# Down-projection by one level of Strassen's scheme, the feed-forward in two passes of 256 tokens, keys and values kept in DRAM

## The reference, cut to what matters

```python
q = layer_norm(query, ln1_g, ln1_b)
qh, kh, vh = split(q @ wq + bq), split(context @ wk + bk), split(context @ wv + bv)
scores = where(allowed, qh kh^T / sqrt(32), -inf)         # 64 context rows
o = softmax(scores) vh
x = query + o @ wo + bo
h = layer_norm(x, ln2_g, ln2_b)
out = x + gelu(h @ w1 + b1) @ w2 + b2                     # w1 512x2048, w2 2048x512
```

## Time and profile before

| | us |
|---|---|
| median of three runs | 1868.11 (1867.82 to 1868.26) |
| span of the profiled execution, the only time that the page gives of it | 1864.5 |
| PE busy in it | 1799.3 (97%) |
| DVE busy | 1247.9 (67%) |
| ACT busy | 640.5 (34%) |
| POOL busy | 443.8 (24%) |

### The profile page before, as it was taken

One profiled execution on the slowest core, in us unless ns is written; L12 is line 12 of the kernel. 1 busy time (PEld: TensorE's weight loads), 2 busy tenths in 40 slices (PEclk: granted clock), 3 DMA queues, 4 the chain that ended last, 5 costly groups with the idle time before them and its releaser, 6 DMA issues.

```text
span 1864.5 us, 26584 instructions
## 1 busy us (share of the span) xinstructions
PE 1799.3 (97%) x10213; PEld 819.6 (44%) x10213; DVE 1247.9 (67%) x1930; ACT 640.5 (34%) x799; POOL 443.8 (24%) x376
## 2 busy tenths in 40 slices
PE   6678899999999999999999999999999999999999
PEld 3233344444444444444444444444444444444444
DVE  6767757667675767757676676757677576866622
ACT  5654424242232424223242422324242232424211
POOL 2523114131320314122141313203141221413200
PEclk8878999999999999999999999999999999999999
DMA  8230232314123241412323131332413133231200
GB/s 288 54 105 12 46 91 46 91 23 79 35 60 77 46 91 23 78 36 57 80 46 91 19 81 38 57 80 46 91 21 77 40 57 79 46 91 19 50 23 23
DMA packets 287738, 116.27 MB, mean 62 GB/s; under 512 B 262616, under 2 KB 264192, under 8 KB 287616
## 3 DMA queue, kind: packets, MB, share of 16 engines
q1 hardware_dynamic: 287616, 114.61, 27.4%
HBM read 31.22 MB, written 16.78 MB: 26 GB/s over the span
## 4 chain that ended last, share of the span: by engine, by line
PE 90%; DVE 5%; POOL 1%; ACT 1%; DMA 1%; issue 1%; SPq 0%; DVEq 0%; ACTq 0%
PE ff_ps L1141 34%; PE ff_ps L1384 34%; PE at_ps L1141 18%; PE at_ps L1298 2%; PE at_ps L1318 1%; DVE w_all L829 1%; POOL arena L560 1%; DVE arena L829 0%; DVE xhat L818 0%; DMA arena<-in_L_xattn_wk 0%; PE ff_ps L1213 0%; DVE arena L1114 0%; DVE arena L1061 0%; PE at_ps L1213 0%; DVE smax L1059 0%
## 5 line engine op out<-in xcount | busy, mean ns | idle before, releaser
L1141 PE MATMUL ff_ps<-arena,w_all 128*128 128x512 f16 x3072 | 701.8, 381 | 2.3 <-DVE arena L829 2.3
L1384 PE MATMUL ff_ps<-w_all,arena 128*128 128x512 f16 x3072 | 698.0, 379 | 0.9 <-DVE arena L829 0.9
L1141 PEld LDWEIGHTS ff_ps<-arena,w_all 128*128 128x128 f16 x3072 | 300.4, 98 | 371.7 <-issue 15.6
L1384 PEld LDWEIGHTS ff_ps<-w_all,arena 128*128 128x128 f16 x3072 | 294.4, 98 | 358.6 <-issue 6.4
L753 ACT ACTIVATE arena<-ff_ps,b1p,scales 128x512 f32<-128x512 f32 x256 | 198.5, 775 | 634.6 <-PE ff_ps L1141 634.3
L1114 DVE TENSOR_SCALAR arena<-arena,scales 128x512 f16<-128x512 f32 x256 | 150.1, 586 | 215.6 <-ACT arena L753 215.5
L829 DVE SCALAR_TENSOR_TENSOR arena<-arena,scales 128x512 f16<-128x512 f32 x256 | 239.2, 934 | 9.1
L511 POOL TENSOR_TENSOR rstd<-ve,minus_half 128x1 f32<-128x1 f32 x128 | 85.6, 669 | 561.1 <-DVE ve L801 561.1
L555 POOL TENSOR_TENSOR x_sb<-x_sb,bo_row 128x512 f32<-128x512 f32 x64 | 92.6, 1477 | 359.8 <-PE at_ps L1298 350.5
L687 ACT ACTIVATE norm_hl<-xhat 128x512 f16<-128x512 f32 x120 | 73.9, 628 | 287.6 <-DVE xhat L818 287.6
L560 POOL TENSOR_TENSOR arena<-arena,rsum 128x1024 f32<-128x1024 f32 x64 | 124.8, 1971 | 176.1 <-DVE rsum L1087 176.1
(11 more groups left out here) (154 smaller groups left out, 1377.3 us busy)
## 6 DMA issues: line engine op xcount, KB each, us to landing
x_sb<-in_x SPq DMA_DIRECT2D x64, 256.0 KB, 2.8
out_x<-arena SPq DMA_DIRECT2D x64, 256.0 KB, 2.1
w_all<-in_L_xattn_w SPq DMA_DIRECT2D x6, 1024.0 KB, 11.6
arena<-in_L_xattn_w SPq DMA_DIRECT2D x2, 1024.0 KB, 15.8
v_sb<-v_sb SPq DMA_DIRECT2D x6, 192.0 KB, 3.0
arena<-in_ctx SPq DMA_DIRECT2D x1, 1024.0 KB, 5.2
arena<-in_L_xattn_wk SPq DMA_DIRECT2D x1, 1024.0 KB, 7.4
arena<-in_L_xattn_wq SPq DMA_DIRECT2D x1, 1024.0 KB, 7.4
```

The lines of the kernel that those rows point to most:

```text
L1141: last = nc.tensor.matmul(out_ap, s, m, start=(i == 0), stop=(i == n - 1))
L1384: last = nc.tensor.matmul(ff2_ps[:, t, :], pair[:, s, rows], m[:, j], start=(j == 0 and i == 0), stop=(j == NJ - 1 and i == 2))
```

## The change

A group of the feed-forward is now two feature tiles by 256 tokens instead of one tile by 512. FF1 of a group is 24 matmuls of 256 columns. Four blocks of 128 x 128 (two tiles, two halves of the 256 tokens) come out of the gelu, which is two ACT instructions of 256 columns into blocks 0, 2, 4, 6 of `comb`. DVE adds three pairs of blocks and subtracts two, so that seven blocks stand there (896 columns); ACT makes their high half by a Copy, DVE their low half. FF2 of a group is the seven products of Strassen's scheme, each of three matmuls with 256 columns: 21 matmuls in the place of 24 of that width. The seven sums gather in four banks, and DVE puts them into the residual by eight instructions for each 256 tokens (`update`), 16 for each slot. The first pass of a slot (groups 0 to 7) is for its first 256 tokens, the second for the others.

w2 is brought in eight pieces of two row blocks into a ring of two stages, POOL adds and subtracts its blocks, and ACT and DVE convert seven blocks of 128 x 256 for each piece, in slot 1, at the positions of `CONV_SECOND_AT`. Its maxima are taken earlier in slot 0. Keys and values go to DRAM in slot 0, and in each odd slot SP loads those of the next batch (six DMAs); the POOL steps that built `kblk` and copied the values are gone but for slot 0. The attention of slots 2 to 15 is planned four positions earlier, with the steps in the same order; slot 1 keeps the old plan.

```diff
 LAG = 3
-GROUPS = NJ + LAG
+NGROUP = NJ
+GROUPS = NGROUP + LAG
+SUBS = 2
+PAIRS = NJ // 2
+SUB = CHUNK // SUBS
+DH = D // 2
+NPROD = 7
+PRODUCTS = ((2, 6, 0, 0), (4, 0, 0, 1), (6, 5, 1, 0), (5, 4, 1, 1), (1, 2, 2, 0), (0, 1, 2, 1), (3, 3, 3, 0))
 PLAN = {
+    3: [("Q", 0), ("Q", 1), ("Q", 2), ("Q", 3)],
+    4: [("S", 0)], 6: [("S", 1)], 7: [("E", 0), ("E", 1)], 8: [("S", 2)],
+    9: [("U", 0), ("U", 1)], 10: [("S", 3)],
+    11: [("Z", 0), ("Z", 1), ("L", 0), ("L", 1), ("E", 2), ("E", 3)],
+    12: [("U", 2), ("U", 3)],
+    14: [("Z", 2)], 15: [("Z", 3), ("L", 2), ("L", 3)],
+    19: [("V", 0), ("V", 1)], 20: [("V", 2), ("V", 3)],
+    21: [("O", 0), ("O", 1)],
+    22: [("G", 0), ("O", 2), ("G", 1), ("D", 0), ("O", 3), ("G", 2), ("D", 1), ("G", 3), ("D", 2), ("D", 3)],
+    23: [("N", 0), ("N", 1), ("N", 2), ("N", 3)],
+    25: [("A", 0), ("A", 1), ("C", 0), ("A", 2)], 26: [("C", 1), ("A", 3), ("C", 2)], 27: [("C", 3)],
+}
+PLAN_LATE = {
...
-W2_SUMS_AT = (19, 20, 21, 22)
+W2_SUMS_AT = (11, 12, 17, 18)
+CONV_SECOND_AT = {1: (12, 13), 2: (14,), 3: (15, 16), 4: (17,), 6: (18, 19), 8: (20, 21), 9: (22, 23),
+                  10: (24, 25), 12: (26, 27), 14: (28, 29), 16: (30, 31), 18: (32, 33), 20: (34, 35)}
...
+            def load_values(batch):
+                for half in (slice(0, SC), slice(SC, P)):
+                    sp.dma_start(v_now[half], v_batches[batch].rearrange("k (a n) -> k a n", a=2)
+                                 ).then_inc(kv_loaded, 16)
+            def load_keys(batch):
+                for q in range(GH):
+                    rows = slice(q * HD, (q + 1) * HD)
+                    sp.dma_start(kblk[rows, :, :, q % 2, :].rearrange("p a g k -> p (a g) k"),
+                                 k_batches[batch, rows, :, :]).then_inc(kv_loaded, 16)
...
+                    if ff:
+                        store_out(c, par, 0)
+                    if par and loads:
+                        sp.wait_ge(v_ps, 4 * c + TT)
...
+                        load_keys(ahead)
+                        load_values(ahead)
...
+                def add_w2(j):
+                    w = stage[j % 2]
+                    pool.wait_ge(w2_staged[j % 2], 32 * (j // 2 + 1))
+                    nc.gpsimd.tensor_tensor(w[:, 1:6:2, :], w[:, 0:5:2, :], w[:, 2:7:2, :], ALU.add
+                                            ).then_inc(pool_adds, 1)
+                    pool.wait_ge(pool_adds, j + 1)
+                    nc.gpsimd.tensor_tensor(w[:, 0:7:6, :], w[:, 0:3:2, :], w[:, 4:7:2, :], ALU.subtract
+                                            ).then_inc(w2_added, 1)
...
# ACT, group g
-                        nc.scalar.activation(gelu_full[g % 2], ff1_ps[:, g % 2, :], ACT.Gelu,
-                                             bias=b1p[:, g:g + 1], scale=col(C1)).then_inc(g_full, 1)
+                        for y in range(2):
+                            ft = 2 * (g % PAIRS) + y
+                            last = nc.scalar.activation(
+                                comb[g % 2][:, 2 * y:2 * y + 5:4, :],
+                                ff1_ps[:, g % 2, y * SUB:(y + 1) * SUB].rearrange("p (m n) -> p m n", n=P), ACT.Gelu,
+                                bias=b1p[:, ft:ft + 1], scale=col(C1))
+                        last.then_inc(g_full, 1)
+                    if ff and 1 <= g <= NGROUP:
+                        act.wait_ge(g_comb, NGROUP * c + (g - NGROUP))
+                        nc.scalar.activation(g_pair[(g - 1) % NG][:, 0], comb[(g - 1) % 2], ACT.Copy, scale=col(SG)
+                                             ).then_inc(g_hi, 1)
...
# DVE, group g
-                        nc.vector.tensor_scalar(pair[:, 0, :], gelu_full[g % 2], col(SG), None, ALU.mult
-                                                ).then_inc(g_hi, 1)
-                        dve.wait_ge(g_hi, NJ * c + (g + 1 - NJ))
-                        low(pair[:, 1, :], gelu_full[g % 2], col(SG), pair[:, 0, :], g_lo)
+                        w = comb[g % 2]
+                        nc.vector.tensor_tensor(w[:, 1:6:2, :], w[:, 0:5:2, :], w[:, 2:7:2, :], ALU.add
+                                                ).then_inc(g_sums, 1)
+                        dve.wait_ge(g_sums, NGROUP * c + (g + 1 - NGROUP))
+                        nc.vector.tensor_tensor(w[:, 0:7:6, :], w[:, 0:3:2, :], w[:, 4:7:2, :], ALU.subtract
+                                                ).then_inc(g_comb, 1)
+                    if ff and 1 <= g <= NGROUP:
+                        dve.wait_ge(g_hi, NGROUP * c + (g - NGROUP))
+                        pair = g_pair[(g - 1) % NG]
+                        low(pair[:, 1], comb[(g - 1) % 2], col(SG), pair[:, 0], g_lo)
+                    if ff and g == PAIRS - 1 + LAG:
+                        update(c, par, 0)
...
# PE, FF1 of group g and FF2 of group j = g - 3
+                        for y in range(2):
+                            ft = 2 * pair + y
+                            cut = slice(ft % KT * P, (ft % KT + 1) * P)
+                            w1_hi, w1_lo = (w1_pairs[:, ft // KT, a] for a in range(2))
+                            last = triple(ff1_ps[:, g % 2, y * SUB:(y + 1) * SUB],
+                                          [((w1_hi[:, k, cut], w1_lo[:, k, cut]), (old[:, 0, k], old[:, 1, k]))
+                                           for k in range(KT)])
...
+                        pe.wait_ge(g_lo, NGROUP * c + (j + 1 - NGROUP))
+                        if pair == 0:
+                            wait(pe, updated, 2 * UPDATES * c + UPDATES * (s - 2))
...
+                        rows, weights = g_pair[j % NG], w2_products[pair]
+                        for m, w, b, half in PRODUCTS:
+                            for i, (r, a) in enumerate(((0, 0), (0, 1), (1, 0))):
+                                last = nc.tensor.matmul(
+                                    ff2_ps[:, b, half * DH:(half + 1) * DH], rows[:, r, m], weights[:, a, w],
+                                    start=(pair == 0 and half == 0 and i == 0), stop=(pair == PAIRS - 1 and i == 2),
+                                    skip_group_check=True)
```

More of the change, by code:

```diff
@@ L303, in cross_attention_block @@
         v_biased = sem("v_biased")
-        v_moved = sem("v_moved")
+        k_stored, v_stored, kv_loaded = (sem(n) for n in ("k_stored", "v_stored", "kv_loaded"))
+        w2_staged = [sem(f"w2_staged{i}") for i in range(2)]
+        w2_added = sem("w2_added")
+        pool_adds = sem("pool_adds")
         x_loaded = [sem(f"x_loaded{t}") for t in range(TT)]
@@ L373, in plan @@
                 return PLAN_FIRST.get(position, [])
-            second = PLAN_SECOND.get(position, []) if isinstance(c, int) and c == 1 else []
-            return PLAN.get(position, []) + second
+            if isinstance(c, int) and c == 1:
+                return PLAN_LATE.get(position, []) + PLAN_SECOND.get(position, [])
+            return PLAN.get(position, [])
         def halves(c, t):
@@ L530, in values_low, with slot @@
                 pool.wait_ge(kv_hi, KT + n + 1)
-                nc.gpsimd.tensor_tensor(v_sb[:, 1, 2 * n], kv_full[n % 2], v_sb[:, 0, 2 * n], ALU.subtract
+                nc.gpsimd.tensor_tensor(v_sb[:, 1, n], kv_full[n % 2], v_sb[:, 0, n], ALU.subtract
                                         ).then_inc(kv_out, 1)
-            def slot(c, par, attn, ff, batch):
+            def slot(c, par, attn, ff, batch, ahead):
                 first = isinstance(c, int) and c == 0
+                second = isinstance(c, int) and c == 1
                 def key_blocks():
                     for a in range(2):
-                        keys = kT_sb[:, a, :, bass.ds(batch * SC, SC)]
+                        keys = kT_sb[:, a, :, 0:SC]
                         nc.gpsimd.tensor_tensor(
@@ L1026, in aside, with slot, update @@
                     convert(n)
-            def slot(c, par, attn, ff, batch):
+            def slot(c, par, attn, ff, batch, ahead):
                 last = isinstance(c, int) and c == NCHUNK - 1
+                def update(c, par, s):
+                    first_row, second_row = (x1[1 - par][:, t] for t in (2 * s + 1, 2 * s))
+                    left, right = slice(0, DH), slice(DH, D)
+                    base = 2 * UPDATES * c + UPDATES * (s - 2)
+                    bank = [ff2_ps[:, b, :] for b in range(4)]
+                    dve.wait_ge(x1b_set, 4 * c + (2 * s - 2))
+                    for n, (b, rows, cut, into, scale) in enumerate((
+                            (0, slice(0, D), slice(0, D), first_row, C2), (0, slice(0, D), slice(0, D), second_row, C2),
+                            (1, slice(0, D), slice(0, D), first_row, C2), (2, slice(0, D), slice(0, D), second_row, C2),
+                            (1, right, left, first_row, NC2), (2, left, right, second_row, NC2),
+                            (3, left, left, first_row, C2), (3, left, right, second_row, C2))):
+                        dve.wait_ge(ff2_done, 8 * c + (4 * s - 8 + b + 1))
+                        if n >= 2:
```

(12 more changed lines are left out.)

323 lines of the change are left out of this document (177 added, 146 removed).

## The result

The kernel after took 2059.51 to 2063.90 us in three runs, median 2061.79; a fourth, at a clock of 0.649, was disturbed and is left out of the comparison. The kernel before, run beside it, had a median of 1867.96. The ratio is 1.1039, interval 1.1024 to 1.1054: slower by a tenth. The prediction was 1955, range 1885 to 2010. It had the sign and the mechanism of the steady slots, and missed the size by 107 us.

What follows compares the result with a forecast made beforehand. PE bound the kernel, with only 1.6 us to spare at V before DVE's longer chain would make it wait. The span summed as 1864.5 + 71 + 18 - 3 = 1950.5, median 3.6 above; predicted 1955, range 1885 to 2010.

Steps and rivals of the forecast that it cites:

- the mechanism of the steady slots: Slots 2 to 15: DVE's longer groups delay the transposes, so PE waits at V, 2 to 5 us in each slot.
- S0 to V: Steady slot, first scores to first V step: DVE's chain grows 5.0 us, the stage goes from 42.4 to 44.6 us.
- Short matmuls: PE's FF1 and FF2: a matmul of 256 columns costs 109.2 ns, so PE's work falls 4.3 us in each slot.
- third rival: PE: a short matmul costs near its upper bound, 11 us more PE work in a slot, 2012 in all; chance 0.06.
- POOL keeps this cost, so I leave it as it is: DVE's chain after S0: hold-ups beside POOL's bias rows stay as before, some 2 us either way for a slot.
- in the odd slot the chain has 2.4 us less work (35.75 - 33.31), so 36.9: DVE's chain from S0 to V: 36.9 us in odd slots, 39.3 in even ones; V starts after 43.4 and 45.8.
- V to S0: Steady slot, V to next scores: waits of 1.1 us at O and 1.8 at the slot's end, 66.5 to 69.4 us.
- second rival: Each slot's wait at V drops the clock to half rate, 2.7 us each, 38 more, 1990 in all; chance 0.18.
- Slots 2 to 15 together: The 14 steady slots: each goes from 108.9 to 114.0 us, 5.1 more, +71 in all.
- about 6 us for seven or eight groups, the first eight updates (4.6), and about 4 for conversions: Slot 1, between S0 and V: what the change adds on an already full DVE, priced at +14 us.
- Slot 0: Four POOL bias rows of 1.48 us stand in front of its last values, in place of two copies: +3 us.
- Slots 15 and 16: Slot 15 has no next norm; slot 16, without attention, gains 4.3 on PE less a longer last update: together -3 us.

Runs made afterwards that it cites:

- e7: Kernel after, V, O and first norms one plan position later, the first eight updates behind V's low halves on DVE: 1996.47 us, a slot 113.92.
- e8: Kernel after with another plan for attention steps and norms, found by walking the program's order with the rows' durations, updates as in e7: 1955.41 us, a slot 111.12.
- e1: Kernel after, each group's add and subtract on DVE cut to 8 of each 128 columns: 2013.53 us, a slot 115.38.
- e5: Kernel after, POOL's eight bias additions of each slot cut to 8 of 512 columns: 2012.71 us, a slot 115.73, slot 1 174.3.
- e3: Kernel after, 36 unused matmuls of 256 columns put ahead of PE's wait at V from slot 2 on: 2038.57 us.
- e2: Kernel after, slot 1's w2 conversions from the second on one group earlier, POOL's sums for them ahead of its normalisations: 2046.38 us, slot 1 164.3.
- e13: On top of e9, POOL's eight bias additions of slot 1 moved behind its normalisations: 1941.08 us, slot 1 163.6.
- e9: Kernel after with e8's plan and e2's earlier conversions of slot 1 together: 1943.23 us, slot 1 167.3, a slot 111.14.

## Why the prediction was right in sign and wrong in size

The steps of the prediction summed to 1950.5 for a span that was 2062.3. Three of them failed: slot 1 was priced as added work where it is a loop of waits (35 us), the clock behind the forecast wait was left out of the sum (28 us), and DVE's chain from S0 to V was priced too short (30 us). Step by step:

- **Short matmuls.** 109.2 ns forecast, 109.2 measured. The third rival is out. The Trainium skill's 81 ns for 128 columns ("TensorE: Matmul & The Clock Gate", "Back-to-back issue gap") would have put an estimated 25 ns on each; the trace shows 2.5 ns over the 106.7 of its columns.
- **The mechanism.** V's wait on the transposes leads the list, 4.0 us for each slot (2 to 5 forecast), then FF2 on `low`, S on the subtract, FF1 on the gelu. e7 and e8 show from two sides that it is this chain: one FF2 more ahead of V gave 4.7 us of each slot back, and with PE's work from S0 to V as it was (412 matmuls) an earlier order of the other engines' steps, there and behind V, gave 7.5.
- **S0 to V: 44.6 forecast, 46.77 measured.** Two terms of DVE's chain failed. The first is "POOL keeps this cost, so I leave it as it is". The first group of slot 4 took 1.62 + 1.37 + 2.15 = 5.14 us, 3.0 more than alone, where the first group before took 3.13 in place of 1.22, 1.9 more. But one group is not the stage. Before, the next group was held up by 2.0 us (the first two lines below), after, by 1.1. The hold-ups can be summed in both traces over the chains of slots 2 to 15 (from DVE's first step behind S0 to the end of its last low half), as each instruction's length over the shortest of its kind in that trace: a mean of 5.2 us before, 6.5 after, 6.2 in e1 and 2.5 in e5. So this term is about 1.3 us of the missing 2.2, and inside the 2 us that the forecast had allowed for it. The Trainium skill ("SBUF — State Buffer", "Who interferes with whom") says that of VectorE and GpSimd, on their shared port pair, the one that comes second waits for the other's whole instruction. e1's 16 columns in 1.13 us agree. The second term is "in the odd slot the chain has 2.4 us less work (35.75 - 33.31), so 36.9". The chain of an odd slot had less work, but it was as long, 34.16 us in slot 5 (the last two lines), because DVE stood idle for 3.3 us of it, partly for PE's scores. After the change the even chain is 40.8 us (39.3 forecast) and the odd one 39.2 (36.9 forecast). No run separates the parts of this.

```profile
507.41 1.57 DVE L1114 TENSOR_SCALAR arena<-arena,scales 128x512 f16<-128x512 f32 x1
509.01 1.64 DVE L829 SCALAR_TENSOR_TENSOR arena<-arena,scales 128x512 f16<-128x512 f32 x1
...
607.17 1.23 DVE L1059 TENSOR_REDUCE smax<-at_ps 128x16 f32<-128x1024 f32 x1 [1.41 <-PE at_ps L1298]
...
638.98 2.35 DVE L829 SCALAR_TENSOR_TENSOR qT<-arena,qT 128x1024 f16<-128x1024 f32 x2
```

- **V to S0: 69.4 forecast, 71.92 measured.** Here the second rival was right: the clock falls behind V in each slot. It put 2.7 us on it; e3 measures 2.0. Without the fall the stage is 69.95, within 0.6 of the forecast. I had taken this for a rival to the forecast when it was an addition to it, at a wait that the forecast itself contained.
- **Slots 2 to 15 together:** +71 forecast, +136 measured; of the 65 missing, 14 x 2.0 = 28 are the clock, 14 x 2.2 = 30 the stage from S0 to V (some 18 of them the longer hold-ups), 14 x 0.55 = 8 the rest of the stage from V to S0.
- **Slot 1: +14 forecast, +48.7 measured,** the largest miss in one slot (35 us). The step that failed is the sum "about 6 us for seven or eight groups, the first eight updates (4.6), and about 4 for conversions": it counted the instructions added to DVE and took them as work, where they are a loop. For w2's later pairs the conversion stands in the very group whose FF2 needs it, behind the gelu of an FF1 that PE issues only after the FF2 before. PE was busy for 55.79 of 95.54 us from S0 to V, at a clock of 0.75, and DVE for only 63.24: neither bounds it by its work. DVE's timeline in slot 1, weights beside the bias additions (two low halves of 1280 columns together, two of 512):

```profile
177.64 4.34 DVE L946 SCALAR_TENSOR_TENSOR w_all<-arena,scales,w_all 128x1280 f16<-128x1280 f32 x2
...
186.92 3.96 DVE L946 SCALAR_TENSOR_TENSOR w_all<-w_all,gs 128x512 f16<-128x512 f32 x2
```

The first took 2.2 and the second 1.4 where POOL was quiet. The order of the conversions is 17 us of the 48.7 (e2), the hold-ups beside the bias additions 7 (e5). The two were not run together on the kernel after; behind the earlier conversions, moving the additions gave 3.7 us (e13 against e9). The other 24 or more hold the 14 that were priced and about 10 that no run here tells apart. One cost among them can be read: five of the eight FF2 from S0 to V, each behind a wait, are 4.6 us long where the last is 2.46, some 11 us in their rows at the half clock. The +14 had no clock in it, and no run held the clock up there.

```profile
260.00 4.64 PE L1528 MATMUL ff_ps<-w_all,arena 128*128 128x256 f16 x21 [5.63 <-DVE w_all L946]
...
267.46 2.46 PE L1528 MATMUL ff_ps<-w_all,arena 128*128 128x256 f16 x21
```

- **Slot 0: +3 forecast, +10.3 measured.** The chain of waits of the kernel after (start, us, what) goes through POOL's bias rows, which took 7.75 us and not 4 x 1.48, and at the end through the load, POOL's sums and DVE's conversion of w2's first pairs, which the step had not named:

```profile
84.13 7.75 POOL x_sb L642 x4
...
109.06 3.04 DMA arena<-in_L_xattn_w
112.17 1.82 POOL arena L660
...
117.95 1.26 POOL arena L663
120.66 1.39 DVE w_all L946 x2
```

This is read from the trace alone; no run tested it.
- **Slots 15 and 16: -3 forecast.** Slot 16 is 2.6 us longer, not shorter. Its trace shows one wait of 2.6 us, of FF2 for the first pass's updates, and a half clock behind it; no run tested it.
